# Weight tiles loaded two per DMA instead of one, in the preparation of a feed-forward stage with binarized weights

## The chip, the cores and the metric

The kernel runs as one program on the 8 cores of one Trainium2 chip. Each core computes one of the eight batch entries, and no data passes between cores. The metric is the device time of the slowest core, in microseconds (us).

## What is computed

Two layers, each of the form x + attention(norm(x)) + ffn(norm(x)), on x of 8 x 4096 x 1024 in float32. Only the feed-forward part of layer 0 matters here. Its weights are replaced by their signs, scaled by the mean absolute value of a row:

```python
def _binarize(w):
    alpha = jax.lax.stop_gradient(jnp.mean(jnp.abs(w), axis=1, keepdims=True))
    bw = alpha * jnp.sign(w)
    return w + jax.lax.stop_gradient(bw - w)
bw1 = _binarize(w1)                                   # w1: 4096 x 1024
h = jnp.einsum('bsd,hd->bsh', x, bw1) + b1
h = jax.nn.gelu(h, approximate=False)
bw2 = _binarize(w2)                                   # w2: 1024 x 4096
out = jnp.einsum('bsh,dh->bsd', h, bw2) + b2
```

## The kernel before

The program is a row of phases, A to G: a layer norm (A), the projection and the attention of layer 0 (B, C), its feed-forward (D), a layer norm (E), and the attention and feed-forward of layer 1 (F, G). Between two phases stands a barrier: every engine waits for all work of the others. The code of each engine is written out in the order in which it runs, and waits are explicit, on semaphores. Phase D is `emit_ffn0`, and the change is in it alone.

Phase D begins with a preparation, in which each core makes the signed weights and their scales. The tables lie transposed in device memory: `w1T` is 1024 x 4096 and `w2T` 4096 x 1024, float32. `w1T` is cut into 8 tiles of 128 rows (128 x 4096), `w2T` into 32 tiles of 128 rows (128 x 1024). Each tile goes through these steps:

- POOL issues a DMA (`sec_wload`, L793 for `w1T` and L801 for `w2T`) that reads the tile from device memory and writes it as bfloat16 into one of four slots of the buffer `d_wraw`. Slot number: tile number modulo 4. A `w2T` tile fills only the first 1024 columns of its slot.
- ACT (`sec_wact`) waits for the landing, writes Sign of the slot to the resident table `sw1T` or `sw2T`, and then replaces the slot by its Abs, in place. These instructions go through a helper that records them all at line L214; the table load of ACT before the first Sign has that line too. Each ACT instruction waits for the one before.
- PE (`sec_alpha_mm`) multiplies a matrix of ones (`d_ones`) by the slot and sums in PSUM (`d_pAw`): eight matmuls of 512 columns for a `w1T` tile (L827), two for a `w2T` tile (L837). They count the semaphore `TE` (called `d_te` in the order of instructions) up, by 8 and by 2 a tile.
- Before POOL issues a tile into a used slot, it waits for `TE` to show that PE has read the tile that was in it: for tile k of `w1T` from the fifth on, that tile k-4 is through. The first four tiles of `w2T` wait for all of `w1T`, since the sums share PSUM; from then on the wait is again for the tile four before.

The landings are counted on four semaphores in turn (`LW`, a `DStream`; `d_lw0` to `d_lw3` in the order of instructions), one issue each. Issue i is waited for on semaphore i modulo 4.

When PE has summed all of `w1T`, DVE writes the scales to `d_a1bc`. POOL, behind its last weight load, sends one row of them to device memory (`a1s`, L857), waits for it, and gathers it back as columns (`d_a1col`, L859). After the sum of `w2T` DVE writes `d_a2bc`. SP loads meanwhile the first chunk of activations (`d_xc`) and rows of the residual (`d_x1p`).

Then the main part of the phase runs, for 8 chunks of 512 tokens: 256 matmuls `d_pH<-d_xc,sw1T` (L917), Gelu on ACT with `d_a1col` as its scale, 256 matmuls `d_pO<-sw2T,d_hC` (L930), and the scaling by `d_a2bc` and the residual on DVE. PE's first matmul of it waits for the chunk, for `d_a1col` and for DVE's two scales. The memory of `d_wraw` is given to `d_hC` there.

Of the kernel before, what the change touches and what calls it, by code (L numbers as in the profile page):

```python
# [18 lines left out]
T = 4096  # L19
NKT = 8  # L20
NTT = 32
NCH = 8
# [736 lines left out]
def emit_ffn0(ctx, xnC_dram, x1p_dram, x1_dram, es):  # L759
# [9 lines left out]
    wraw = ctx.sb("d_wraw", [128, 4 * T], BF16, es_prep)  # L769
# [4 lines left out]
    dw1T, dw2T = ctx.t["d_w1T"], ctx.t["d_w2T"]  # L774
    xnCv_dram = xnC_dram.rearrange("p (k t) -> p k t", k=NKT)

    LW = DStream(ctx, "d_lw", nbuf=4)
# [9 lines left out]
    bl.vector(sec_ones)  # L787

    def sec_wload(gpsimd):
        for k in range(NKT):  # L790
            if k >= 4:
                gpsimd.wait_ge(TE.h, (k - 3) * NCH)
            LW.issue(gpsimd.dma_start(out=wraw[:, (k % 4) * T:(k % 4 + 1) * T],  # L793
                                      in_=dw1T[k * 128:(k + 1) * 128, :]))
        for jt in range(NTT):
            r = NKT + jt
            if jt < 4:
                gpsimd.wait_ge(TE.h, NKT * NCH)
            else:
                gpsimd.wait_ge(TE.h, NKT * NCH + (jt - 3) * 2)  # L800
            LW.issue(gpsimd.dma_start(out=wraw[:, (r % 4) * T:(r % 4) * T + 1024],  # L801
                                      in_=dw2T[jt * 128:(jt + 1) * 128, :]))
    bl.gpsimd(sec_wload)

    def sec_wact(scalar):
        scalar = SS(scalar, SE)
        for k in range(NKT):
            w = wraw[:, (k % 4) * T:(k % 4 + 1) * T]
            LW.wait_done(scalar, k)
            scalar.activation(out=sw1T[:, k * T:(k + 1) * T], in_=w,  # L810
                              func=AF.Sign)
            scalar.activation(out=w, in_=w, func=AF.Abs)
        for jt in range(NTT):
            r = NKT + jt
            w = wraw[:, (r % 4) * T:(r % 4) * T + 1024]
            LW.wait_done(scalar, r)
            scalar.activation(out=sw2T[:, jt * 1024:(jt + 1) * 1024],
                              in_=w, func=AF.Sign)
            scalar.activation(out=w, in_=w, func=AF.Abs)
    bl.scalar(sec_wact)  # L820

    def sec_alpha_mm(tensor):
# [929 lines left out]
```

## Time and profile before

| what | us |
|---|---|
| runs of the kernel | 3905.52 and 4174.64, median 4040.08 |
| the execution that was profiled | 3909.16 |
| span of its slowest core (core 6) | 3907.6 |
| spans of the eight cores | 3883.0 to 3907.6 |
| busy in that span: PE, DVE, ACT, POOL | 2940.2, 1438.2, 939.0, 98.9 |

The profile is of one execution, on the slowest core. PE is TensorE's matmuls, PEld its weight loads, DVE is VectorE, ACT ScalarE, POOL GpSimd and SP SyncE. Times in its timeline count from the start of the span. "Idle before" an instruction is given in square brackets with what ended it; a bracket is missing where it was idle for next to nothing. A landing is the time from the issue of a DMA to the increment that reports it. "L214" is the helper's line, so that groups there are told apart by their tiles.

### The profile page before, as it was taken

The page shows a single profiled execution, that of the slowest core. Times are in us where ns is not written, and L with a number is a line of the kernel's source. Part 1 is how long each engine was busy: PE and PEld are TensorE (multiplying, and loading weights), DVE is VectorE, ACT ScalarE, POOL GpSimd, SP SyncE. Part 2 cuts the span into 40 slices and gives each one's busy share as a digit, 9 for nine tenths or more (in the row PEclk, how much of TensorE's full clock was granted, in tenths as well). Part 3 has the DMA queues.
Part 4 walks back from the last instruction along what each step waited for, and adds up shares of the span by engine and source line. Part 5 has one row for each costly group of instructions (what it writes and reads, how often), then busy time and mean ns, then how long its engine had stood idle before and what let it go on. Part 6 is the DMA issues. An engine that isn't in the chain of part 4 may idle for free.

```text
span 3907.6 us, 40898 instructions; the slowest of 8 cores (3883.0 to 3907.6 us)
## 1 busy us (share of the span) xinstructions
PE 2940.2 (75%) x14101; PEld 1345.7 (34%) x14368; DVE 1438.2 (37%) x1387; ACT 939.0 (24%) x1061; POOL 98.9 (3%) x193
## 2 busy tenths in 40 slices
PE   2398999999999448999999994152214737898987
PEld 1144444444444203444444442121101312333333
DVE  7204333333333100011110004799994214544443
ACT  5232222222222483221112222420000002111210
POOL 0000000000000010000000000000000010000000
PEclk9999999999999759999999996576657968999999
DMA  4611111111111560111111113600015881211212
GB/s 146 167 54 28 33 33 42 35 33 33 33 37 39 104 95 17 44 54 55 54 54 44 39 38 114 189 11 22 22 43 154 263 161 36 73 60 60 65 44 76
DMA packets 137256, 264.15 MB, mean 68 GB/s; under 512 B 41808, under 2 KB 83040, under 8 KB 135008
## 3 DMA queue, kind: packets, MB, share of 16 engines
q1 hardware_dynamic: 114624, 194.89, 16.8%
q0 software_dynamic: 22432, 66.63, 7.6%
q8 instruction: 121, 1.98, 0.2%
q14 instruction: 79, 0.65, 0.1%
HBM read 202.22 MB, written 92.29 MB: 75 GB/s over the span
## 4 chain that ended last, share of the span: by engine, by line
PE 63%; DVE 19%; DMA 7%; ACT 5%; issue 4%; SPq 1%; DVEq 0%; POOL 0%; ACTq 0%; PEldq 0%; POOLq 0%; PEld 0%
PE d_pH L917 11%; PE d_pO L930 11%; PE c_pe L581 11%; PE c_pO L612 8%; PE g_pO L1370 6%; PE g_pL L1403 5%; PE b_pf L503 3%; PE c_pO L621 3%; DVE f_Pc L214 2%; PE f_pO L1274 2%; DMA f_rbT<-rC_h 2%; DVE f_tmp L214 2%; DVE f_Qc L214 2%; DVE e_st L214 1%; DVE f_sin L214 1%
## 5 line engine op out<-in xcount | busy, mean ns | idle before, releaser
L581 PE MATMUL c_pe<-fC 128*128 128x512 bf16 x2015 | 448.1, 381 | 14.2 <-ACT e_sb L680 8.0
L930 PE MATMUL d_pO<-sw2T,d_hC 128*128 128x512 bf16 x2007 | 441.2, 379 | 11.5 <-ACT d_hC L214 9.3
L917 PE MATMUL d_pH<-d_xc,sw1T 128*128 128x512 bf16 x2008 | 443.5, 381 | 5.2 <-DMA d_a1col<-a1s 3.0
L214 ACT ACT_TABLE_LOAD x86 | 110.3, 1283 | 1157.0 <-PE g_pL L1403 386.5
L612 PE MATMUL c_pO<-fT,aT_sb 128*128 128x512 bf16 x1472 | 338.9, 379 | 40.5 <-ACT aT_sb L668 38.7
L214 ACT ACTIVATE d_hC<-d_pH,b_col_sb,d_a1col 128x512 bf16<-128x512 f32 x256 | 198.9, 777 | 637.7 <-PE d_pH L917 637.7
L1403 PE MATMUL g_pL<-g_xc,WinTb 128*128 128x512 bf16 x1192 | 276.7, 386 | 87.8 <-DMA g_xc<-xn1C_h 62.5
L963 DVE TENSOR_TENSOR d_x1o<-d_pO,d_a2bc 128x1024 f32<-128x1024 f32 x32 | 39.2, 1225 | 820.0 <-PE d_pO L930 820.0
L581 PEld LDWEIGHTS c_pe<-fC 128*128 128x128 bf16 x2048 | 200.2, 98 | 256.9 <-issue 17.1
L930 PEld LDWEIGHTS d_pO<-sw2T,d_hC 128*128 128x128 bf16 x2048 | 199.4, 98 | 253.3 <-issue 13.1
L917 PEld LDWEIGHTS d_pH<-d_xc,sw1T 128*128 128x128 bf16 x2048 | 200.3, 98 | 247.7 <-issue 7.2
L1132 PE MATMUL f_pV<-xn1C,Wvo 128*128 128x512 bf16 x501 | 123.1, 408 | 214.9 <-ACT f_v L214 181.2
L1370 PE MATMUL g_pO<-WoutTb,g_msk 128*128 128x512 bf16 x1192 | 278.6, 379 | 4.0 <-DVE g_msk L214 2.7
L1274 PE MATMUL f_pO<-Wvo,f_rbT 128*128 128x512 bf16 x502 | 127.5, 410 | 159.4 <-DMA f_rbT<-rC_h 155.5
L612 PEld LDWEIGHTS c_pO<-fT,aT_sb 128*128 128x128 bf16 x1536 | 145.0, 97 | 195.9 <-issue 36.9
L680 ACT COPY e_sb<-c_pe 128x512 f32<-128x512 f32 x128 | 74.9, 585 | 532.7 <-PE c_pe L581 532.3
L1403 PEld LDWEIGHTS g_pL<-g_xc,WinTb 128*128 128x128 bf16 x1216 | 114.9, 99 | 248.4 <-issue 127.0
L727 DVE COPY e_sb<-c_pe 128x512 f32<-128x512 f32 x128 | 88.5, 691 | 301.0 <-PE c_pe L581 292.3
L1370 PEld LDWEIGHTS g_pO<-WoutTb,g_msk 128*128 128x128 bf16 x1216 | 118.4, 97 | 146.9 <-issue 3.2
L731 DVE TENSOR_REDUCE c_st<-e_sb 128x1 f32<-128x4096 f32 x32 | 141.4, 4419 | 26.0 <-POOL e_sb L214 26.0
L1132 PEld LDWEIGHTS f_pV<-xn1C,Wvo 128*128 128x128 bf16 x512 | 52.4, 103 | 285.4 <-issue 234.2
L656 ACT ACTIVATE a_sb<-e_sb,c_st 128x4096 bf16<-128x4096 f32 x32 | 118.7, 3708 | 119.2 <-DVE c_st L731 119.2
(116 smaller groups left out, 2588.3 us busy)
## 6 DMA issues: line engine op xcount, KB each, us to landing
c_xr<-x SPq DMA_DIRECT2D x32, 512.0 KB, 5.0
x1p_h<-c_x1p SPq DMA_DIRECT2D x32, 512.0 KB, 5.8
d_x1p<-x1p_h SPq DMA_DIRECT2D x32, 512.0 KB, 4.4
x_h<-d_x1o SPq DMA_DIRECT2D x32, 512.0 KB, 5.2
f_x1r<-x_h SPq DMA_DIRECT2D x32, 512.0 KB, 5.8
x2p_h<-f_x2p SPq DMA_DIRECT2D x32, 512.0 KB, 6.7
g_x2p<-x2p_h SPq DMA_DIRECT2D x32, 512.0 KB, 3.9
out<-g_out POOLq DMA_DIRECT2D x32, 512.0 KB, 4.5
```

Of the source, the lines that this page charges most:

```text
L214: ins = f(*a, **k)
L503: ins = tensor.matmul(pf[:, (r % 2) * 512:(r % 2 + 1) * 512], Wb[:, k * 1024 + j * 128:k * 1024 + (j + 1) * 128], xchunk[:, (q % 2) * NKT ...
L581: ins = tensor.matmul(pe_[:, (r % 2) * 512:(r % 2 + 1) * 512], fC[:, k * T + s * 128:k * T + (s + 1) * 128], fC[:, k * T + q * 512:k * T + ...
L612: tensor.matmul(pO[:, (sp % 2) * 1024 + q2 * 512:(sp % 2) * 1024 + (q2 + 1) * 512], aT_sb[:, i * 128:(i + 1) * 128], fT[:, i * 1024 + q2 * ...
L656: ch.do(SEx, lambda sc, s=s: sc.activation(out=a_sb[:, (s % 2) * T:(s % 2 + 1) * T], in_=e_sb[:, (s % 2) * T:(s % 2 + 1) * T], func=AF.Exp ...
L731: ch.do(VEm, lambda v, s=s: v.reduce_max(out=cst[:, (s % 2):(s % 2) + 1], in_=e_sb[:, (s % 2) * T:(s % 2) * T + T], axis=AX.X, negate=True))
L917: ins = tensor.matmul(pH[:, (r % 2) * 512:(r % 2 + 1) * 512], sw1T[:, k * T + jt * 128:k * T + (jt + 1) * 128], xchunk[:, xoff + k * 512:x ...
L930: ins = tensor.matmul(pO[:, (i % 2) * 1024 + dc * 512:(i % 2) * 1024 + (dc + 1) * 512], hC[:, jt * 512 + sub * 128:jt * 512 + (sub + 1) * ...
L1132: ins = tensor.matmul(pV[:, (m % 2) * 512:(m % 2 + 1) * 512], Wvo[:, dt_ * 1024 + k * 128:dt_ * 1024 + (k + 1) * 128], xn1C[:, dt_ * T + q ...
L1274: ins = tensor.matmul(pO[:, (b % 2) * 1024 + q2 * 512:(b % 2) * 1024 + (q2 + 1) * 512], rbT[:, (b % 2) * 1024 + k * 128:(b % 2) * 1024 + ( ...
L1370: ins = tensor.matmul(pO[:, (i2 % 2) * 1024 + dc * 512:(i2 % 2) * 1024 + (dc + 1) * 512], msk2[:, moff + jt * 512 + sub * 128:moff + jt * ...
L1403: ins = tensor.matmul(pL[:, (jt % 2) * 512:(jt % 2 + 1) * 512], WinTb[:, k * JW + jt * 128:k * JW + (jt + 1) * 128], xchunk[:, xoff + k * ...
```

## The change

POOL's loads take two tiles each. A DMA of `w1T` covers 256 rows and fills two neighbouring slots, a DMA of `w2T` covers 256 rows too and fills the first 1024 columns of two neighbouring slots. So there are 4 + 16 DMAs in place of 8 + 32. Before a pair is issued, POOL waits until PE has read both tiles that lay in the two slots. ACT's wait for tile k is now one for the pair k // 2, and the landings of pairs are counted on the four semaphores in turn. The instructions of ACT, PE and DVE are the same, in the same order.

```diff
@@ -787,33 +787,41 @@
     bl.vector(sec_ones)
 
     def sec_wload(gpsimd):
-        for k in range(NKT):
+        for p in range(NKT // 2):
+            k = 2 * p
             if k >= 4:
-                gpsimd.wait_ge(TE.h, (k - 3) * NCH)
-            LW.issue(gpsimd.dma_start(out=wraw[:, (k % 4) * T:(k % 4 + 1) * T],
-                                      in_=dw1T[k * 128:(k + 1) * 128, :]))
-        for jt in range(NTT):
+                gpsimd.wait_ge(TE.h, (k - 2) * NCH)
+            LW.issue(gpsimd.dma_start(
+                out=wraw[:, (k % 4) * T:(k % 4 + 2) * T].rearrange(
+                    "p (s c) -> p s c", s=2),
+                in_=dw1T[k * 128:(k + 2) * 128, :].rearrange(
+                    "(s p) c -> p s c", p=128)))
+        for pq in range(NTT // 2):
+            jt = 2 * pq
             r = NKT + jt
             if jt < 4:
                 gpsimd.wait_ge(TE.h, NKT * NCH)
             else:
-                gpsimd.wait_ge(TE.h, NKT * NCH + (jt - 3) * 2)
-            LW.issue(gpsimd.dma_start(out=wraw[:, (r % 4) * T:(r % 4) * T + 1024],
-                                      in_=dw2T[jt * 128:(jt + 1) * 128, :]))
+                gpsimd.wait_ge(TE.h, NKT * NCH + (jt - 2) * 2)
+            LW.issue(gpsimd.dma_start(
+                out=wraw[:, (r % 4) * T:(r % 4 + 2) * T].rearrange(
+                    "p (s c) -> p s c", s=2)[:, :, 0:1024],
+                in_=dw2T[jt * 128:(jt + 2) * 128, :].rearrange(
+                    "(s p) c -> p s c", p=128)))
     bl.gpsimd(sec_wload)
 
     def sec_wact(scalar):
         scalar = SS(scalar, SE)
         for k in range(NKT):
             w = wraw[:, (k % 4) * T:(k % 4 + 1) * T]
-            LW.wait_done(scalar, k)
+            LW.wait_done(scalar, k // 2)
             scalar.activation(out=sw1T[:, k * T:(k + 1) * T], in_=w,
                               func=AF.Sign)
             scalar.activation(out=w, in_=w, func=AF.Abs)
         for jt in range(NTT):
             r = NKT + jt
             w = wraw[:, (r % 4) * T:(r % 4) * T + 1024]
-            LW.wait_done(scalar, r)
+            LW.wait_done(scalar, NKT // 2 + jt // 2)
             scalar.activation(out=sw2T[:, jt * 1024:(jt + 1) * 1024],
                               in_=w, func=AF.Sign)
             scalar.activation(out=w, in_=w, func=AF.Abs)
```

POOL's queue in phase D, from the first weight load to the gather of the scales (minus is before, plus is now; the names are out<-in):

```order
-L793 DMA d_wraw<-w1T 128x4096 x4
-L793 DMA d_wraw<-w1T 128x4096 [waits d_te] x4
-L801 DMA d_wraw<-w2T 128x1024 [waits d_te] x32
-L863 UNCONDITIONAL_BRANCH
-L857 DMA a1s<-d_a1bc 16x1x256 [waits d_ve]
-L859 DMA d_a1col<-a1s 128x32x1 [waits d_a1l]
+L811 UNCONDITIONAL_BRANCH [waits bar_sy,bar_te,bar_ve,bar_se]
+L794 DMA d_wraw<-w1T 128x2x4096 x2
+L794 DMA d_wraw<-w1T 128x2x4096 [waits d_te] x2
+L806 DMA d_wraw<-w2T 128x2x1024 [waits d_te] x16
+L871 UNCONDITIONAL_BRANCH
+L865 DMA a1s<-d_a1bc 16x1x256 [waits d_ve]
```

The loads have become half as many with twice the bytes; the two small transfers behind them stand where they stood (the last one, the gather to `d_a1col`, is cut off at the end of the rows).

ACT's queue at the start of the same preparation; `d_lw0` to `d_lw3` count landings, `d_se` is ACT's own order:

```order
 L214 ACTIVATE sw1T<-d_wraw 128x4096 [waits d_lw0]
 L214 ACTIVATE d_wraw<-d_wraw 128x4096 [waits d_se]
+L214 ACTIVATE sw1T<-d_wraw 128x4096 [waits d_lw0,d_se]
+L214 ACTIVATE d_wraw<-d_wraw 128x4096 [waits d_se]
 L214 ACTIVATE sw1T<-d_wraw 128x4096 [waits d_lw1,d_se]
 L214 ACTIVATE d_wraw<-d_wraw 128x4096 [waits d_se]
+L214 ACTIVATE sw1T<-d_wraw 128x4096 [waits d_lw1,d_se]
+L214 ACTIVATE d_wraw<-d_wraw 128x4096 [waits d_se]
 L214 ACTIVATE sw1T<-d_wraw 128x4096 [waits d_lw2,d_se]
```

The instructions are the same. The second tile now waits on the semaphore of the first, since both come with one DMA, and the third on the one that was the second's.

## Rows read from the trace of the kernel before

**Rows 1.** The page's part 2, busy tenths in 40 slices of 97.7 us.
```profile
PE   2398999999999448999999994152214737898987
...
ACT  5232222222222483221112222420000002111210
```

**Rows 2.** The cores' spans: the slowest.
```profile
core 6: 3907.6 us, clock 0.900
```

**Rows 3.** The chain that ended last, in time: start us, us, what.
```profile
1314.49 39.11 DMA d_wraw<-w1T
...
1353.74 3.63 ACT sw1T L214
...
1394.99 5.17 DMA d_wraw<-w2T
```

**Rows 4.** Timeline of core 6, the w1T part: start us, us, instruction, idle before it.
```profile
1312.88 2.17 POOL L793 DMA_DIRECT2D d_wraw<-w1T  x4 [40.38 <-SPq L276]
...
1325.74 1.28 ACT L214 ACT_TABLE_LOAD   x1 [35.19 <-DMA d_wraw<-w1T]
...
1337.04 3.62 ACT L214 ACTIVATE sw1T<-d_wraw 128x4096 bf16<-128x4096 bf16 x1 [2.68 <-DMA d_wraw<-w1T]
...
1353.74 3.62 ACT L214 ACTIVATE sw1T<-d_wraw 128x4096 bf16<-128x4096 bf16 x1 [1.25 <-DMA d_wraw<-w1T]
...
1356.65 0.53 POOL L793 DMA_DIRECT2D d_wraw<-w1T  x1 [7.49 <-PE d_pAw L827]
...
1365.33 0.53 POOL L793 DMA_DIRECT2D d_wraw<-w1T  x1 [8.15 <-PE d_pAw L827]
...
1387.11 3.62 ACT L214 ACTIVATE d_wraw<-d_wraw 128x4096 bf16<-128x4096 bf16 x1
```

**Rows 5.** The waits between 1300 and 1480 us: total, times, longest.
```profile
ACT sw1T L214 <- DMA d_wraw<-w1T: 4.7, 3, 2.7
```

**Rows 6.** Landings of w1T's DMAs issued first and second, at 1356.65, at 1365.33.
```profile
DMA to landing us min/median/max: 12.8/18.1/23.5
...
DMA to landing us min/median/max: 18.1/18.1/18.1
...
DMA to landing us min/median/max: 15.4/15.4/15.4
```

**Rows 7.** Timeline, the w2T part: its start, and one slot in steady running.
```profile
1394.99 2.12 POOL L801 DMA_DIRECT2D d_wraw<-w2T  x4 [29.13 <-PE d_pAw L827]
...
1400.30 1.06 ACT L214 ACTIVATE sw2T<-d_wraw 128x1024 bf16<-128x1024 bf16 x1 [9.57 <-DMA d_wraw<-w2T]
...
1454.25 1.06 ACT L214 ACTIVATE d_wraw<-d_wraw 128x1024 bf16<-128x1024 bf16 x1
...
1457.01 0.53 POOL L801 DMA_DIRECT2D d_wraw<-w2T  x1 [1.77 <-PE d_pAw L837]
```

**Rows 8.** Landings of w2T's DMAs: the first two issued, and those from 1404 to 1466.5.
```profile
DMA to landing us min/median/max: 5.2/5.8/6.5
...
DMA to landing us min/median/max: 3.6/4.8/5.2
```

**Rows 9.** One stretch: us, busy PE, PEld, DVE, ACT, POOL; PEclk, DMA share, GB/s.
```profile
1404.00:1466.00 62.00, 26.95 (x53) 3.67 (x54) 0.00 (x0) 57.05 (x55) 14.28 (x27) 0.50 0.79 110
```

**Rows 10.** Timeline, the end of the preparation.
```profile
1466.70 0.51 POOL L857 DMA_DIRECT2D a1s<-d_a1bc  x1
...
1471.78 1.74 POOL L859 DMA_DIRECT2D d_a1col<-a1s  x1 [4.57 <-DMA a1s<-d_a1bc]
...
1472.61 1.06 ACT L214 ACTIVATE d_wraw<-d_wraw 128x1024 bf16<-128x1024 bf16 x1
...
1475.00 1.22 DVE L214 TENSOR_SCALAR d_a2bc<-d_pAw 128x1024 bf16<-128x1024 f32 x1 [75.95 <-PE d_pAw L837]
...
1477.80 2.72 PE L917 MATMUL d_pH<-d_xc,sw1T 128*128 128x512 bf16 x6 [2.98 <-DMA d_a1col<-a1s]
```

**Rows 11.** Landings of Wb's DMAs, 256 KB each, the first two issued.
```profile
DMA to landing us min/median/max: 8.8/9.3/9.9
```


## The prediction

> **What bounds the kernel now.** I read the page's slices first. PE is busy in nine tenths of most slices; one of the holes is the fourteenth and fifteenth slices, where PE shows 4 and 4, and ACT 4 and 8 [rows 1]. At 97.7 us a slice these are 1270 to 1465 us, and the hole is the place between layer 0's attention and its feed-forward, the preparation of the signed weights, and it is the only place that the change touches. The span of core 6, the slowest, is 3907.6 us [rows 2]; the execution that left the trace took 3909.16 us.
>
> Next the chain of waits for that place. It begins with a landing of `w1T` (39.11 us of DMA), then runs on ACT from 1353.74, then the eight matmuls that end `w1T`, one landing of `w2T`, and ACT again to the end [rows 3]. So in the first 41 us the DMA decides, and afterwards ACT decides nearly alone. The timeline says how closely. The four prefetched tiles are issued together at 1312.88; ACT starts at 1325.74, waits 2.68 us for the second tile and 1.25 us for the fourth, and from 1353.74 it never waits again until 1390.73 (1387.11 + 3.62), five tiles at 7.42 us [rows 4]. All waits of `sw1T` on DMA after the first are 4.7 us [rows 5]. In the `w2T` part ACT waits 9.57 us once, for the first tile [rows 7], and then goes from 1400.30 to 1473.67 (1472.61 + 1.06 [rows 10]) with no wait: 73.37 us for 32 tiles, 2.293 each.
>
> What keeps ACT fed is worth a look. A slot is issued again 4.26 us after Abs ends in the `w1T` part (1390.73 to 1394.99) and 1.70 us after it in the `w2T` part (1454.25 + 1.06 to 1457.01) [rows 4, 7]: PE has to read the slot in between. A tile then lands in 4.8 us (median) [rows 8]. With four slots there are 3 x 2.293 = 6.88 us between Abs's end and the slot's next use, of which 1.70 + 4.8 = 6.5 are needed. The cover is 0.4 us thick. At the end, PE's first `d_pH` matmul waits for neither ACT nor DVE but for the small gather `d_a1col`, issued by POOL at 1471.78 behind all the weight loads, 4.13 us after ACT's last Abs [rows 10].
>
> **The change, part by part.** Same bytes, same ACT and PE work, same four slots. What moves is the grain: 20 DMAs of two tiles in place of 40 of one; ACT's first Sign of a pair waits until both tiles have landed; and a pair is issued only when PE has read both tiles of the pair before it in those slots. So four single buffers become two double ones. A pair's slots are free from its own Abs until the other pair is through ACT, so what was three tiles of time for an issue and a landing is one pair, two tiles of time, and the landing is that of twice the bytes. Behind ACT's wait for a pair stand all its later Signs and Abs; PE's sums wait for Abs, POOL's next issue for PE's sums, and behind POOL's loads stands the gather. So a late pair delays the whole stage by as much.
>
> *Start of `w1T`.* Pair 0 lands when the second tile did, since the same bytes move in the same queue. The second tile's landing is 23.5 us after an issue at about 1313.5 [rows 6], and ACT resumed at 1337.04 [rows 4]. The table load (1.30 us with its gap) stands between the landing and the first Sign, so Sign starts at 1338.34 in place of 1327.04. Two tiles take 14.84 us; Abs of the second ends at 1353.10. Pair 1 has landed at 1353.6, as the fourth tile did (1314.49 + 39.11 [rows 3]), so ACT goes on at 1353.74, as before, but with tile 2 and not tile 3. That is one tile behind, 7.4 us, already.
>
> *Pair 2 and pair 3.* Pair 2 is issued at 1353.10 + 4.26 = 1357.36, where before already tile 6 was out at 1356.65 [rows 4]. No row shows a pair of `w1T` from an idle queue. From below: landings at the end of the part follow each other in 1374.75 to 1380.73, 6.0 us (1356.65 + 18.1 and 1365.33 + 15.4 [rows 4, 6]), and the part of a landing that is not transfer is 5.2 us less 1.8 us, 3.4 us, from the first two tiles of `w2T` (landed at 1394.99 + 5.2 = 1400.2 and, issued a quarter of 2.12 us later, at 1395.52 + 6.5 = 1402.0 [rows 7, 8]); 3.4 + 2 x 6.0 = 15.4 us. From above: the first two tiles, issued beside SP's loads, took 24.0 us. I take the mean pace, (1380.73 - 1337.0) / 6 = 7.3 us a tile, so 18.0 us. Then:
> pair 2 lands at 1375.4, while ACT is through with tile 3 at 1368.5, a wait of 6.8 us; tiles 4 and 5 last to 1390.2; pair 3, issued at 1368.5 + 4.26 = 1372.8, lands at 1390.8; the last Abs ends at 1390.8 + 14.76 = 1405.5. Before it was 1390.73: **+14.8 us**. With 15.4 us the same steps give +12.2, with 24.0 us +20.8.
>
> *Start of `w2T`.* The same 4.26 us to the issue, then pair 0 lands at the second tile's 1402.0 in place of 1400.2 (a tile of 5.2, a pair of 7.0 us) [rows 7, 8]. **+1.7 us**.
>
> *The rest of `w2T`.* A pair takes ACT 2 x 2.293 = 4.59 us. Its slots are issued 1.70 us later, and the next pair in them lands after L. A buffer's round is 4.59 + 1.70 + L, and holds two pairs, which ACT alone would do in 9.17 us. L is not in the trace either. From an idle queue it was 7.0 us from the first issue. In steady running the DMA engines are busy 0.79 of the time [rows 9], so a tile of 2.293 us needs 1.8 us of them, and a second tile behind the first makes 4.8 + 1.8 = 6.6 us. I take 6.8. Round: 13.09 us, 3.92 us over 9.17. After pairs 0 and 1 there are seven rounds: **+27.4 us**. Bounds: L of a single tile, 4.8 us, gives 1.92 a round and +13.4; twice a single landing, 9.6 us, gives 6.72 and +47.0. Below nothing it can't go: for that L would have to be under 2.9 us, and the fastest single tile took 3.6 [rows 8]. The waits should come every second pair: pair 2n lands late, pair 2n+1, issued 4.6 us after it, is there in time.
>
> *The tail.* POOL issues `a1s` behind its last weight load, and that stands in the same place in its queue. But the last pair is issued 13.1 - 1.7 = 11.4 us before ACT's end, where it was 7.5 us, so `a1s` and `d_a1col` (0.53, then up to 6.3 behind the pair, 0.6, then 5.9 us) are through by 15.1 us after pair 13's Abs, and DVE's `d_a2bc`, which ends 2.55 us after the last Abs (1473.67 to 1476.22 [rows 10]), by 15.6. PE starts 2.6 us after Abs instead of 4.13: **-1.5 us**.
>
> *At nothing.* POOL's issues halve (2.12 us for four [rows 7]), but POOL waits most of this time, and a pair's issue is inside L. Semaphores of landings rotate as before, one wait in place of one. SP's queue is not passed by anything: its chunk and rows have until PE's first `d_pH`. Nothing in the later stages moves, except that all come later.
>
> Here a rule speaks for the change. The traced landings show a part that doesn't grow with the bytes (3.4 us by rows 7 and 8). The Trainium skill, "DMA: Bandwidth & Descriptors", section "Anatomy of one DMA — SWDGE (gpsimd) path", says the same in a formula, 2.0 us fixed and the bytes at 436 GB/s, and its rules tell authors to coalesce. By that formula an estimate for a pair of `w2T` is 3.2 us counted by what is written and 4.4 us by what is read, and the seven rounds would cost 2 to 11 us in place of 27. The trace agrees on there being a fixed part, and not on the pace: single tiles here need 4.8 us with the engines at 0.79.
>
> Sum: 14.8 + 1.7 + 27.4 - 1.5 = **+42.4 us**, on 3909.2, so **3951.6 us**, 1.1% more. The two runs shown are 3905.52 and 4174.64 us with a median of 4040.08; the profiled execution stands by the lower. The forecast is on that footing; what makes the upper run longer no row shows, and it is left out of the sum.
>
> **The rivals.**
> A. *Only the waiting for both tiles costs.* A pair lands hardly later than a tile, as the engines have 0.21 of their time free in steady running and more when ACT stalls. With L = 4.8 and 15.4 us for `w1T`: 12.2 + 0 + 13.4 - 1.5 = +24.1, 3933.3 us. For it: some single landings took only 3.6 us. Against it: the fourfold issue at 1394.99 shows tiles landing 1.8 us apart.
> B. *Coalescing pays for itself, no slower.* Should the fixed part be nearly all of a landing, pair 0 would land with the first tile, 12.8 us [rows 6], ACT's 4.7 us of waits in `w1T` would go, and each later pair would take the 12.8 and 3.6 us of the best single tiles. Then pair 2, issued at 1346.1, lands at 1358.9, 2.2 us late, pair 3 in time, `w1T` ends 2.2 us earlier; the rounds cost 0.72 x 7 = 5.0; with the tail +1.3, 3910.5 us. It takes a pair of 2 tiles in 12.8 us where the trace took 24. The skill's page above is the rule that it would follow.
> C. *Slower by more than 2%.* A pair could land much later than its bytes ask, because two rows per partition come less well in step on the 16 engines or because memory is shared with seven cores at the same instant. The nearest row: two tiles of `Wb` of the same size, issued together, landed after 0.5 + 9.9 = 10.4 us [rows 11]. With L = 10.4 a round is 16.69, +52.6 over seven; the start of `w2T` +5.1 (10.4 in place of 5.3); `w1T` at 24.0 us +20.8: sum with no gain in the tail 78.5, 3987.7 us. 2% is 78 us, so this decides from L of about 10.4 us, twice a single tile's.
>
> **How the numbers follow.** Forecast 0.72: its own range, with L of 6 to 8 us (+22 to +36) and `w1T` of +12.2 to +20.8, is about 3943 to 3967 us. A 0.14. B 0.05. C 0.09, of which rather more than half lies above 2%. The range reaches from just under A to just under C: 3930 to 3985 us. A change of 2% is about what a measurement of this kernel can tell from none. Slower by over 2%: 0.06, from C. Faster by over 2% (78 us) would need more than the whole 14 us that ACT waits for landings here: 0.01. Within 2%: 0.93.
>
> **What would show the steps.** In the profile after: first Sign of `sw1T` near 1338; one wait of ACT on `w1T` of 5 to 13 us before tile 4 and a small one before tile 6; last Abs of `w1T` near 1405; in the `w2T` part seven waits of ACT of some 3.9 us, every second pair, 27 us in all, and landings of pairs of 6 to 8 us; PE's first `d_pH` near 1520 with DVE `d_a2bc` or the gather as its releaser within a microsecond of each other; everything after it shifted and else alike. No waits of ACT in `w2T` would refute the main term; waits at every pair, or a longer landing, would make it larger; a shift of another stage by more than a few microseconds would mean that I have missed something outside of the preparation.

## The result

The changed kernel ran in 3939.34 us (median), the kernel before, on the same chips, in 3905.22 us. The ratio is 1.0088 with a 95% interval of 1.0076 to 1.0099, so the change costs 34 us, 30 to 39. It is slower beyond doubt, by less than 2%. The time is inside the range of 3930 to 3985 us, and below the 3943 to 3967 us that the prediction called the forecast's own. The forecast, 3951.6 us, is 12 us too high: 8 us in the change (+42.4 for +34), and 4 us in what it is added to, 3909.2 us, where the kernel before now ran in 3905.2. Medians are over all executions, ratios leave out those that a slower state of the chip disturbed, and of the one disturbed execution that is read below (pairs in the w2T part alone, 4189 us) only the preparation is used.

### The profile page after: what moved, and what is told of

Its sections match the earlier page's. It is cut to its first block, busy times and chain, and to the rows that moved or that the text cites. A ratio compares the mean times of both kernels' runs of the same rounds, so it can differ in the third digit from the quotient of the medians.

```text
span 3935.5 us, 41127 instructions; the slowest of 8 cores (3903.4 to 3935.5 us)
## 1 busy us (share of the span) xinstructions
PE 2960.5 (75%) x14368; PEld 1348.2 (34%) x14368; DVE 1438.5 (37%) x1387; ACT 939.6 (24%) x1061; POOL 92.0 (2%) x173
## 4 chain that ended last, share of the span: by engine, by line
PE 63%; DVE 19%; DMA 8%; ACT 4%; issue 4%; SPq 1%; DVEq 0%; ACTq 0%; POOL 0%; POOLq 0%
PE c_pe L581 11%; PE d_pO L938 11%; PE d_pH L925 11%; PE c_pO L612 9%; PE g_pO L1378 6%; PE g_pL L1411 5%; PE b_pf L503 3%; PE c_pO L621 3%; DVE f_Pc L214 2%; DVE f_tmp L214 2%; DVE f_Qc L214 2%; PE f_pO L1282 2%; DMA f_rbT<-rC_h 2%; DVE e_st L214 1%; DVE f_sin L214 1%
## 5 line engine op out<-in xcount | busy, mean ns | idle before, releaser
L612 PE MATMUL c_pO<-fT,aT_sb 128*128 128x512 bf16 x1536 | 347.1, 379 | 32.3 <-ACT aT_sb L668 32.3
L1140 PE MATMUL f_pV<-xn1C,Wvo 128*128 128x512 bf16 x512 | 123.1, 405 | 214.7 <-ACT f_v L214 181.9
```

The source lines that it names most:

```text
L612: tensor.matmul(pO[:, (sp % 2) * 1024 + q2 * 512:(sp % 2) * 1024 + (q2 + 1) * 512], aT_sb[:, i * 128:(i + 1) * 128], fT[:, i * 1024 + q2 * ...
L1140: ins = tensor.matmul(pV[:, (m % 2) * 512:(m % 2 + 1) * 512], Wvo[:, dt_ * 1024 + k * 128:dt_ * 1024 + (k + 1) * 128], xn1C[:, dt_ * T + q ...
```

## The profile after

The profiled execution took 3937.04 us, against 3909.16 before. Its slowest core is core 3. The page's slices, PE and ACT, as [rows 1]:

```profile
PE   2398999999999337999999995243313737898997
...
ACT  5232222222222365211122222421100002111210
```

PE's fourteenth and fifteenth slices fell from 4 and 4 to 3 and 3, ACT's from 4 and 8 to 3 and 6: the same work over a longer hole. The chain that ended last, from the first load to PE's first `d_pH`, on core 3 (start us, us, what), which answers to [rows 3]:

```profile
1309.57 25.44 DMA d_wraw<-w1T
1335.08 1.28 ACT L214
...
1355.38 15.75 DMA d_wraw<-w1T
1371.27 3.62 ACT sw1T L214
...
1404.83 6.38 DMA d_wraw<-w2T
1411.35 1.07 ACT sw2T L214
...
1417.56 7.20 DMA d_wraw<-w2T
1424.89 1.07 ACT sw2T L214
...
1431.10 6.42 DMA d_wraw<-w2T
...
1443.86 5.43 DMA d_wraw<-w2T
...
1455.64 5.80 DMA d_wraw<-w2T
...
1467.78 6.21 DMA d_wraw<-w2T
...
1480.33 5.70 DMA d_wraw<-w2T
...
1492.38 5.75 DMA d_wraw<-w2T
```

Before, one landing of `w1T` and one of `w2T` were in it. Now there are two of `w1T` and, of `w2T`, the first and then seven more, 5.4 to 7.2 us each, 6.1 on the mean. ACT's waits for landings, of the same core:

```profile
ACT sw2T L214 <- DMA d_wraw<-w2T: 33.8, 8, 10.5
ACT sw1T L214 <- DMA d_wraw<-w1T: 5.3, 1, 5.3
```

The eight of `sw2T` are the first, 10.5 us, and seven of 3.3 us on the mean; they come at every second pair. For `sw1T` there is one, before the fifth tile. The timeline shows how one round comes about:

```profile
1411.35 1.06 ACT L214 ACTIVATE sw2T<-d_wraw 128x1024 bf16<-128x1024 bf16 x1 [10.51 <-DMA d_wraw<-w2T]
...
1419.39 1.06 ACT L214 ACTIVATE d_wraw<-d_wraw 128x1024 bf16<-128x1024 bf16 x1
1424.89 1.06 ACT L214 ACTIVATE sw2T<-d_wraw 128x1024 bf16<-128x1024 bf16 x1 [4.45 <-DMA d_wraw<-w2T]
...
1417.56 0.71 POOL L806 DMA_DIRECT2D d_wraw<-w2T  x1 [11.30 <-PE d_pAw L845]
1422.15 0.72 POOL L806 DMA_DIRECT2D d_wraw<-w2T  x1 [3.88 <-PE d_pAw L845]
1431.10 0.71 POOL L806 DMA_DIRECT2D d_wraw<-w2T  x1 [8.24 <-PE d_pAw L845]
```

The second Abs of pair 0 ends at 1415.87, POOL issues into its slots at 1417.56, 1.69 us later, ACT is through with pair 1 at 1420.45, and the pair lands only at 1424.8. Pair 3, issued at 1422.15, is in time. The end of the preparation, as [rows 10]:

```profile
1496.97 0.71 POOL L806 DMA_DIRECT2D d_wraw<-w2T  x1 [3.88 <-PE d_pAw L845]
1497.68 0.52 POOL L865 DMA_DIRECT2D a1s<-d_a1bc  x1
...
1502.92 1.73 POOL L867 DMA_DIRECT2D d_a1col<-a1s  x1 [4.72 <-DMA a1s<-d_a1bc]
...
1506.30 1.06 ACT L214 ACTIVATE d_wraw<-d_wraw 128x1024 bf16<-128x1024 bf16 x1
...
1508.69 1.22 DVE L214 TENSOR_SCALAR d_a2bc<-d_pAw 128x1024 bf16<-128x1024 f32 x1 [99.81 <-PE d_pAw L845]
1510.27 2.29 PE L925 MATMUL d_pH<-d_xc,sw1T 128*128 128x512 bf16 x5 [1.76 <-DVE d_a2bc L214]
```

PE's matmul is released by DVE's `d_a2bc` and no longer by the gather (on cores 1 and 6 it is still the gather). It starts 2.9 us after the last Abs.

The same reading on all eight cores gives the balance. The numbers are means over the cores, in us, from the timelines:

| stretch | before | after | difference | forecast |
|---|---|---|---|---|
| first issue of `w1T` to the table load | 11.3 | 23.2 | +11.9 | +11.3 |
| first issue to last Abs of `w1T` | 75.8 | 88.2 | +12.5 | +14.8 |
| from there to the first Sign of `w2T` | 8.1 | 9.7 | +1.6 | +1.7 |
| first Sign to last Abs of `w2T` | 73.8 | 94.5 | +20.7 | +27.4 |
| last Abs to PE's first `d_pH` | 4.4 | 3.0 | -1.4 | -1.5 |
| first issue to PE's first `d_pH` | 162.1 | 195.4 | +33.4 | +42.4 |

The first row is a part of the second; the last is the sum of the other four. It agrees with the 34 us of the timed runs. From PE's first `d_pH` to the end of the span the mean of the cores is 2422.0 us before and 2419.5 after, and the first issue came 2.2 us earlier after the change. The code of these stages is the same, so this is taken for the difference between two executions; because of it the mean span grew by only 28.7 us between the two profiles.

## The experiments

Each kernel was timed against the kernel before on the same chip, in five rounds. "Stage" is the last row of the table above for that kernel, 162.1 us before and 195.4 with the change. The "w2T part" is the time from the last Abs of `w1T` to the last Abs of `w2T`, 81.9 us before and 104.2 with the change. The edits are against the kernel before, except where it is said otherwise, and are cut at "...".

### Pairs in the w1T part alone

```diff
-                gpsimd.wait_ge(TE.h, (k - 3) * NCH)
-            LW.issue(gpsimd.dma_start(out=wraw[:, (k % 4) * T:(k % 4 + 1) * T],
+                gpsimd.wait_ge(TE.h, (k - 2) * NCH)
+            LW.issue(gpsimd.dma_start(
+                out=wraw[:, (k % 4) * T:(k % 4 + 2) * T].rearrange(
+                    "p (s c) -> p s c", s=2),
...
-            LW.wait_done(scalar, k)
+            LW.wait_done(scalar, k // 2)
```

> Pairs in the w1T part alone; w2T with single DMAs as before. From before to after, the mean over the eight cores grew by 12.5 us from the first issue to the last Abs of w1T, by 22.4 us in the w2T part, and shrank by 1.4 us behind it. Theory (lost lead, the two parts add up): 12 us slower than before in all, the w1T part 88 us from first issue to last Abs as in the changed kernel (76 before), the w2T part 82 us as before. Rival (the delay of w1T is taken up by w2T, or the two parts are coupled by the queue): under 5 us slower.

Measured: ratio 1.0020 (1.0005 to 1.0034), 8 us. `w1T` ends 86.6 us after the first issue, the `w2T` part takes 82.3 us, the stage 173.3, 11.3 us more than before. The waits on its slowest core:

```profile
ACT L214 <- DMA d_wraw<-w1T: 47.1, 1, 47.1
ACT sw2T L214 <- DMA d_wraw<-w2T: 9.1, 3, 8.8
ACT sw1T L214 <- DMA d_wraw<-w1T: 4.1, 1, 4.1
```

`sw1T` has its late start and one wait, and `w2T` hardly more than its first wait of 8.8 us, as before. The loss of `w1T`, 10.8 us here, is passed on whole; nothing behind takes it up.

### Pairs in the w2T part alone

```diff
-                gpsimd.wait_ge(TE.h, NKT * NCH + (jt - 3) * 2)
-            LW.issue(gpsimd.dma_start(out=wraw[:, (r % 4) * T:(r % 4) * T + 1024],
+                gpsimd.wait_ge(TE.h, NKT * NCH + (jt - 2) * 2)
+            LW.issue(gpsimd.dma_start(
+                out=wraw[:, (r % 4) * T:(r % 4 + 2) * T].rearrange(
+                    "p (s c) -> p s c", s=2)[:, :, 0:1024],
...
-            LW.wait_done(scalar, r)
+            LW.wait_done(scalar, NKT + jt // 2)
```

> Pairs in the w2T part alone. Theory: w1T part 76 us as before; seven waits of ACT of 2.5 to 4 us at every second pair of w2T, the part 104 us in place of 82; 21 us slower than before in all. Rival (the waits of w2T come from w1T's DMAs or SP's loads being late): w2T without the seven waits, under 5 us slower.

Measured: ratio 1.0043 (1.0031 to 1.0056), 17 us. `w1T` ends at 76.5, the `w2T` part takes 102.5 us, the stage 181.9, 19.9 more than before. The waits of its core 0:

```profile
ACT sw2T L214 <- DMA d_wraw<-w2T: 30.2, 11, 11.0
ACT sw1T L214 <- DMA d_wraw<-w1T: 4.7, 3, 1.7
```

Eleven waits here in place of the eight, since on some cores the delay spreads over both pairs of a round; after the first they sum to 19.2 us on this core and 20.3 on the mean of the cores, where the changed kernel has 21.9. 11.3 and 19.9 make 31.2 of the change's 33.4 us: but for 2 us the two parts add up, and neither needs the other.

### Single DMAs, slots given back two at a time

```diff
-                gpsimd.wait_ge(TE.h, (k - 3) * NCH)
+                gpsimd.wait_ge(TE.h, (k - k % 2 - 2) * NCH)
...
-                gpsimd.wait_ge(TE.h, NKT * NCH + (jt - 3) * 2)
+                gpsimd.wait_ge(TE.h, NKT * NCH + (jt - jt % 2 - 2) * 2)
```

> DMAs of one tile with landings of their own, but POOL gives slots back two at a time, by the waits of the changed kernel. Theory that both the later issue and the later landing cost: in w2T a round is 4.59 + 1.70 + about 4.2 for one tile's landing = 10.5 us, 1.3 over 9.17, so 9 us in seven rounds; in w1T next to nothing, since the issue at about 36 us after the first still finds the queue full; 9 to 10 us slower than before. Rival 1 (the pair's release alone is the loss): 30 us or more slower. Rival 2 (only the pair's landing is the loss): no more than 2 us slower.

Measured: ratio 1.0031 (1.0016 to 1.0047), 12 us; the stage 171.5, 9.4 more than before. `w1T` ends at 75.1, as before. First Sign to last Abs of `w2T` is 85.4 us, against 73.8 before and 94.5 with pairs. The waits on its slowest core:

```profile
ACT sw2T L214 <- DMA d_wraw<-w2T: 22.0, 8, 7.5
ACT sw1T L214 <- DMA d_wraw<-w1T: 2.4, 2, 1.8
```

So the later issue by itself makes 11.6 us of the 20.7 in `w2T`, and the landing of both tiles in one DMA the other 9.1. In `w1T` it is otherwise: giving slots back in pairs costs nothing. On the mean of the cores the fifth tile was issued 33.1 us after the first issue in place of 24.1 and landed at 44.4 us in place of 44.8, behind the tiles that were still on their way. The 12.5 us come all with the landing of both tiles. Both rivals fall.

### Pairs, with sixteen narrow slots for w2T

Against the changed kernel:

```diff
-    LW = DStream(ctx, "d_lw", nbuf=4)
+    LW = DStream(ctx, "d_lw", nbuf=8)
...
-            if jt < 4:
+            if jt < 16:
                 gpsimd.wait_ge(TE.h, NKT * NCH)
             else:
-                gpsimd.wait_ge(TE.h, NKT * NCH + (jt - 2) * 2)
+                gpsimd.wait_ge(TE.h, NKT * NCH + (jt - 14) * 2)
             LW.issue(gpsimd.dma_start(
-                out=wraw[:, (r % 4) * T:(r % 4 + 2) * T].rearrange(
-                    "p (s c) -> p s c", s=2)[:, :, 0:1024],
+                out=wraw[:, (jt % 16) * 1024:(jt % 16 + 2) * 1024].rearrange(
+                    "p (s c) -> p s c", s=2),
```

> Pairs everywhere as in the changed kernel, but the w2T tiles lie 1024 columns apart, so that the same buffer holds 16 tiles, eight pairs, in place of two. Same bytes per DMA. Theory (lost lead): the seven waits of ACT in w2T vanish, what stays is w1T's 12.5 us and 1.6 us for the first pair: 12 us slower than before, 21 us faster than the changed kernel. Rival (a pair's DMA as such is slow, or waiting for both tiles costs at every pair): the waits stay, 30 us or more slower than before.

Measured: ratio 1.0034 (1.0014 to 1.0053), 13 us; the stage 174.3, 12.2 more than before. The waits on its slowest core:

```profile
ACT sw2T L214 <- DMA d_wraw<-w2T: 11.5, 1, 11.5
ACT sw1T L214 <- DMA d_wraw<-w1T: 4.5, 2, 4.2
```

One wait in `w2T`, the first, and then 32 tiles without any, in 73.4 us. The DMAs carry the same bytes as those of the changed kernel. With more of them on their way at once a single one lands later than there (7.6 to 26.7 us from the third pair on, all cores), and yet ACT never waits. What cost time was not the pair as such; it was asked for too late.

### Single DMAs, two slots for w2T

```diff
-            if jt < 4:
+            if jt < 2:
...
-                gpsimd.wait_ge(TE.h, NKT * NCH + (jt - 3) * 2)
-            LW.issue(gpsimd.dma_start(out=wraw[:, (r % 4) * T:(r % 4) * T + 1024],
+                gpsimd.wait_ge(TE.h, NKT * NCH + (jt - 1) * 2)
+            LW.issue(gpsimd.dma_start(out=wraw[:, (jt % 2) * T:(jt % 2) * T + 1024],
```

> Single DMAs, but the w2T tiles use two of the four slots only. Nothing is paired. Theory (the lead between a slot's release and its next use is what counts, whatever the size of the DMA): a round of two tiles is 2.29 of ACT + 1.70 to the issue + 3.6 to 4.2 for the landing of one tile in a queue that is mostly empty = 7.6 to 8.2 us in place of 4.59, 15 rounds, so the w2T part is 45 to 54 us longer than before (82) and longer than with pairs (104). Rival (pairing as such is the loss): under 22 us slower than before.

Measured: ratio 1.0121 (1.0104 to 1.0139), 47 us; the `w2T` part takes 129.0 us, 47.1 more than before. The waits on its slowest core:

```profile
ACT sw2T L214 <- DMA d_wraw<-w2T: 58.6, 28, 8.7
```

With nothing paired the loss is larger than with pairs. The same sum holds for both: ACT's time for a buffer, 1.7 us to the issue, the landing. Here that is 2.29 + 1.70 + 3.6 us (the mean landing from the third tile on) = 7.6 us a round, and 15 rounds lose 3.0 us each, 45 of the 47 us.

### Four tiles per DMA, sixteen slots, the first ones issued early

```diff
-        for jt in range(NTT):
-            r = NKT + jt
-            if jt < 4:
-                gpsimd.wait_ge(TE.h, NKT * NCH)
+        for g in range(NTT // 4):
+            jt = 4 * g
+            if g < 4:
+                gpsimd.wait_ge(TE.h, (g + 5) * NCH)
             else:
-                gpsimd.wait_ge(TE.h, NKT * NCH + (jt - 3) * 2)
-            LW.issue(gpsimd.dma_start(out=wraw[:, (r % 4) * T:(r % 4) * T + 1024],
-                                      in_=dw2T[jt * 128:(jt + 1) * 128, :]))
+                gpsimd.wait_ge(TE.h, NKT * NCH + (jt - 12) * 2)
+            LW.issue(gpsimd.dma_start(
+                out=wraw[:, (jt % 16) * 1024:(jt % 16 + 4) * 1024].rearrange(
+                    "p (s c) -> p s c", s=4),
+                in_=dw2T[jt * 128:(jt + 4) * 128, :].rearrange(
+                    "(s p) c -> p s c", p=128)))
...
-            LW.wait_done(scalar, r)
...
+            LW.wait_done(scalar, NKT + jt // 4)
```

> w1T with single DMAs as before. w2T with four tiles per DMA, so 8 DMAs of 1024 KB, in 16 slots of 1024 columns; and the first four of them are issued as soon as the w1T tile in their place has been read, not after all of w1T. Theory (large DMAs cost nothing where the lead covers them, and the wait of 8.1 us between w1T and w2T is only late issue): no wait of ACT in w2T, none before it; last Abs at 75.8 + 73.5 = 149 us after the first issue, PE's first d_pH 2.9 us later at 152 in place of 162; 10 us faster than before. Rival (waiting for four tiles costs at each DMA): waits of ACT at every fourth tile, no faster than before.

Measured: ratio 0.9982 (0.9972 to 0.9992), 7 us faster than before; the stage 152.6, 9.5 less. The waits on its slowest core:

```profile
ACT L214 <- DMA d_wraw<-w1T: 36.1, 1, 36.1
ACT sw1T L214 <- DMA d_wraw<-w1T: 4.3, 3, 2.1
PE d_pH L920 <- DVE d_a2bc L214: 1.8, 1, 1.8
```

There is no row for `sw2T` at all: ACT's first Sign of `w2T` follows 0.1 us after the last Abs of `w1T`. The DMAs are twice as large as the change's and cost nothing. Of the 9.5 us, 8.0 are the wait before `w2T` (8.1 us before, 0.1 now) and 1.5 the tail. Single DMAs with sixteen slots and the same early issue were not run, so whether the size of the DMAs gives anything of its own is open.

### The same, with Abs on DVE

Against the kernel of the experiment before; PE's waits go to the new semaphore `AB`:

```diff
             scalar.activation(out=sw1T[:, k * T:(k + 1) * T], in_=w,
                               func=AF.Sign)
-            scalar.activation(out=w, in_=w, func=AF.Abs)
...
+            raw.wait_ge(SE.h, k + 1)
+            va.scalar_tensor_tensor(out=w, in0=w, scalar=-1.0, in1=w,
+                                    op0=ALU.mult, op1=ALU.max)
```

> As the kernel with four tiles per DMA and the early issue, and Abs made on DVE, as max(w, -w), behind ACT's Sign. Theory (from the fourth tile on ACT's 7.42 and 2.29 us a tile set the pace of the preparation): ACT's share falls to 3.7 and 1.15 us a tile, so that the landings set the pace, 7.3 us for 1024 KB: 16 such take 117 us from their start, and PE's first d_pH comes 130 to 140 us after the first issue, 22 to 32 us faster than before. Rival (DMA was already the bound, or DVE's Abs is as slow as ACT's pair of instructions): no more than 10 us faster than before, as the kernel with four tiles per DMA.

Measured: ratio 0.9925 (0.9908 to 0.9942), 29 us faster than before; the stage is 128.6 us, 33.4 less than before and 1.4 under the expected 130 to 140. Groups of waits and one stretch, the whole stage, on its slowest core (us, busy PE, PEld, DVE, ACT, POOL; PEclk, DMA share, GB/s):

```profile
ACT sw1T L214 <- DMA d_wraw<-w1T: 28.0, 7, 5.6
ACT sw2T L214 <- DMA d_wraw<-w2T: 18.6, 8, 5.9
```

```profile
1314.80:1446.70 131.90, 59.55 (x129) 12.45 (x130) 80.16 (x42) 64.02 (x41) 12.47 (x18) 0.55 0.86 144
```

```profile
1312.90:1477.80 164.90, 59.31 (x125) 12.60 (x129) 5.65 (x2) 126.75 (x81) 23.44 (x42) 0.55 0.71 115
```

The second stretch is the same stage of the kernel before, on its core 6. ACT was busy 126.75 of 164.90 us and waited little; now it is busy 64.02 of 131.90 and waits at every landing, and the DMA engines went from 0.71 to 0.86 of the time. In the experiment before, with the same DMAs, ACT was busy the same 126.75 us (of 154.6, on its core 7) and the DMA engines 0.71. ACT was the bound of the stage; the landings are it now. This kernel beats the kernel before and the changed one.

### The changed kernel, with w1T's first two tiles single

Against the changed kernel:

```diff
-        for p in range(NKT // 2):
+        for k in range(2):
+            LW.issue(gpsimd.dma_start(out=wraw[:, k * T:(k + 1) * T],
+                                      in_=dw1T[k * 128:(k + 1) * 128, :]))
+        for p in range(1, NKT // 2):
...
-            LW.wait_done(scalar, k // 2)
+            LW.wait_done(scalar, k if k < 2 else k // 2 + 1)
```

> The changed kernel, but w1T's first two tiles come with DMAs of their own, so that ACT's first Sign need not wait for the second tile. In the changed kernel the first Sign is 11.8 us later than before (mean of the cores), and there is one more wait of 5 us at the third pair. Theory 1 (the late first Sign is one loss of 7 us and the late third pair another of 5): w1T ends 7 us sooner than in the changed kernel, at 81 us after the first issue. Theory 2 (ACT only catches up with the landings of the pairs behind, so the late start hides under them): ACT through with the second tile at 31.5 us, tiles 2 and 3 landed as a pair at 40 to 41, the next pair issued at 36 and landed at 54 to 56, the last one issued at 60 and landed at 75, so last Abs at 88 to 91 us, no better than the changed kernel's 88. In both, the w2T part stays at 104 us.

Measured: ratio 1.0081 (1.0066 to 1.0096), 32 us; the stage 190.3, 5.1 us less than the changed kernel's. The timed ratios of the two, 1.0081 and 1.0088, don't tell them apart. `w1T` ends at 84.2 us, between the two theories' 81 and 88, so neither is right. ACT's timeline on its slowest core:

```profile
1326.34 1.28 ACT L214 ACT_TABLE_LOAD   x1 [36.28 <-DMA d_wraw<-w1T]
...
1336.20 3.62 ACT L214 ACTIVATE sw1T<-d_wraw 128x4096 bf16<-128x4096 bf16 x1 [1.24 <-DMA d_wraw<-w1T]
...
1349.96 3.62 ACT L214 ACTIVATE sw1T<-d_wraw 128x4096 bf16<-128x4096 bf16 x1 [6.44 <-DMA d_wraw<-w1T]
...
1366.51 3.62 ACT L214 ACTIVATE sw1T<-d_wraw 128x4096 bf16<-128x4096 bf16 x1 [1.81 <-DMA d_wraw<-w1T]
...
1384.25 3.62 ACT L214 ACTIVATE sw1T<-d_wraw 128x4096 bf16<-128x4096 bf16 x1 [3.00 <-DMA d_wraw<-w1T]
```

ACT starts 12 us sooner than in the changed kernel and then waits 6.4 us for the pair (2, 3), 1.8 for the next and 3.0 for the last. Of the 11.9 us only 4.0 are kept; the rest moves into waits for the pairs behind (12.6 us of waits in `sw1T` in place of 4.7, means of the cores), which Theory 2 had said of all of it. Its error is at the pair (2, 3), for which it had 40 to 41 us after the first issue: that landed at 36.1 on the mean of the cores, and at 35.4 in the changed kernel. From there the way is fixed: 36.1, two tiles on ACT (14.8) and 4.3 to the last issue, which comes at 55.2; its landing at 69.4; two more tiles, 84.2. In the changed kernel the pair (2, 3) lies ready at 35.4 and ACT comes to it only at 39.3 (23.2 + 1.3 + 14.8), so the last issue comes at 58.2. An earlier start can win little more than these 3 to 4 us; the rest of it was hidden under the landing of the pair (2, 3).

## Why the prediction was right in the mechanism and wrong in size

- **That it gets slower, and where.** Right. All of the 33.4 us are between the first weight load and PE's first `d_pH`, and the stages after did not change.
- **Start of `w1T`.** Right: ACT starts 11.9 us later on the mean of the cores, 23.2 in place of 11.3, against 11.3 us later in the working. The core of the profile needed 25.4 us, where 24.0 had been read.
- **Pair 2 and pair 3.** Pair 2 made ACT wait 5.3 us on core 3, against 6.8 forecast; pair 3 was in time there and on four other cores, and 0.3 to 1.8 us late on three. All waits of `sw1T` are 4.7 us on the mean of the cores. The step that was off is "I take the mean pace, (1380.73 - 1337.0) / 6 = 7.3 us a tile, so 18.0 us": the landing of pair 2 was 15.8 us on core 3 and 14.7 on the mean of the cores, at or under the lower bound of 15.4. That makes +12.5 in place of +14.8.
- **Start of `w2T`, +1.7, and the tail, -1.5.** Both as worked out, +1.6 and -1.4, the second with DVE as the releaser on six of the eight cores. The 5.2 and 7.0 us behind the first of them are those of core 6, the slowest of the eight there: the first tile of `w2T` landed in 3.4 to 4.4 us on the others, and the first pair in 5.2 us (median of the cores) in place of the 7.0. Both were read from one core and are too long by the same 1.7 to 1.8 us, so their difference came out.
- **The rest of `w2T`.** The loss is there, and on core 3 with seven waits, every second pair, as said. The step that failed by size, and the larger part of the error, is "so a tile of 2.293 us needs 1.8 us of them, and a second tile behind the first makes 4.8 + 1.8 = 6.6 us. I take 6.8": a pair on the chain landed in 6.1 us on core 3 and 5.8 on the mean of the cores. The 4.8 us was the landing of a tile in a queue that was 0.79 busy. In the changed kernel the queue is less loaded (0.53 on core 3 from 1417 to 1497). The kernel with two single slots shows what that does: with the DMA engines at 0.44 to 0.47 from 1420 to 1460 a single tile landed in 3.6 us. A round was 12.5 us on core 3, (1492.38 - 1417.56) / 6, and 12.2 on the mean, in place of 13.09. Of the 9.0 us by which the sum was too long for the stage this is 6.7, and pair 2 the other 2.3.
- **"A change of 2% is about what a measurement of this kernel can tell from none."** Wrong. The two times shown before, 3905.52 and 4174.64, suggested it, but with 10 and 11 executions the interval is 0.23% wide, and a loss of 0.88% is far outside of it. Together with 0.93 on "within 2%" the sentence says that no change would be told from none, while the prediction's own sum said +1.1%. The sum deserved the belief.
- **Rival A**, +24.1 us, needed a pair to land as fast as a tile; the pair's rounds cost 20.7 us in seven and not 13.4. Its +12.2 us for `w1T` came true. The truth, +33.4, lies half-way between A and the forecast. **Rival B** is out: the first pair of `w1T` landed with the second tile, at 23.1 us where that had landed at 21.2 (means of the cores), and not with the first at 11.2. The kernel with four tiles per DMA does not speak for B, since its gain is the wait before `w2T` and the tail. **Rival C** is out: in steady running a pair landed in 5.0 to 7.4 us on all cores and not in 10.4.
- **The rule on coalescing.** The first landings of `w2T` show a part that doesn't grow with the bytes: 3.5 us for one tile and 5.2 for a pair (medians of the cores) leave 1.8 us of it, where the prediction had 3.4 from core 6. Four tiles per DMA are free with enough slots. But the change goes the way of the rule and loses. The Trainium skill, "DMA: Bandwidth & Descriptors", section "Rules for kernel authors", also says to issue early and wait late; that is the rule that the change broke, and the run that gives slots back in pairs prices the late issue in `w2T` at 11.6 us.

## What to carry to other kernels

Count the lead of a ring of buffers in time: what its other buffers keep the consumer busy for, against the release, the issue and the landing. A ring of four singles and a ring of two doubles hold the same bytes, and the second has a third less lead and needs a longer landing. Before DMAs are made larger, make the ring deep enough for them; narrow slots where the tiles are narrow do it without a byte of memory. And where a consumer engine is the bound, look at moving one of its two instructions to an idle engine: here that was worth 24 us of the stage, where the loads had 9.5 to give. It was tried only on top of the sixteen slots. With four slots of single tiles the three other buffers would keep a faster ACT busy for half as long, 3.4 us for the 6.5 that issue and landing need (an estimate from 3 x 1.15 us), so the gain would probably be smaller there; that was not run.

## What was not expected

- POOL's issue of a DMA over two tiles is recorded with 0.71 us, over four tiles with 0.74, and over one tile with 0.53. The number of tiles hardly matters, the step from one to more does, or that from a plain to a split access pattern; which of the two was not tried.
- The waits of a round need not stay at the first pair. On core 3 they were at every second pair to the end; on core 4 they became fourteen small ones (0.3 to 2.9 us) with nearly the same sum, 21.2 against 23.3 us.
